# One-hot matrices of two MoE routings: eight blocks by one broadcast comparison on VectorE, the products with the codes on GpSimd

## The chip, the cores and the metric

The kernel runs on one core of a Trainium2 chip. The metric is the device time of one execution in microseconds (us). The engines of the core that matter here are TensorE (PE, with its weight loads PEld), VectorE (DVE), ScalarE (ACT), GpSimd (POOL) and the queues that issue DMAs (SP's, and POOL's for indirect ones). Each runs its own list of instructions in order; they meet through semaphores.

## The reference

Two transformer-like layers in a row on x of shape [2, 2048, 128], each half followed by a residual and a layer norm:

```python
x = layernorm(x + deltanet(x))          # layer 0: short convolution, 4 heads, chunks of 64
x = layernorm(x + moe_top1(x))          # 8 experts, GELU, width 512: only the chosen expert counts
x = layernorm(x + linear_attention(x))  # layer 1: 16 heads, causal, no softmax
x = layernorm(x + moe_top2(x))          # 8 experts, SiLU gate * up, width 256, the two largest logits
```

In `moe_top1` a token's output is that of the expert with the largest router logit, times its softmax probability; in `moe_top2` it is the sum over the two chosen experts, weighted by the softmax of their two logits.

## The kernel before

There are 4096 tokens, in `BLOCKS` = 32 blocks of 128. A token lies in a partition, a block in a column. Both mixtures of experts work on sorted tokens: `single_experts` (layer 0) makes `TILES` = 39 tiles of 128 rows, each of one expert; `stage_pairs` (layer 1) makes `GR` = 46 tiles, each of two halves of 64 rows, each half of one pair of experts. Before its tiles can be computed, each finds out which token goes into which row of which tile. That is the routing. It runs once in each layer, while almost nothing else runs:

1. VectorE finds the expert (or the pair) of each token and writes a selection matrix `sel`; TensorE counts tokens by expert and block (`ps_count`), VectorE and TensorE turn the counts into the place of each token, `slot`.
2. VectorE splits `slot` into a tile number `col` and a row in the tile `pos` (L1237 to L1239, L2114 to L2116).
3. For each of the 32 blocks VectorE writes two small matrices with one row per token: `at_pos`, one-hot over 128 rows, and `at_col`, the token's number (`code`) in the column of its tile and 0 elsewhere (39 or 46 columns). TensorE multiplies the two and adds up over the blocks in `ps_found`, which then holds, for each row of each tile, the number of its token. This loop is the one that the diff rewrites:

```python
for n in range(BLOCKS):
    v.tensor_scalar(at_pos[:, n], pos_no[:, :], pos[:, n:n + 1], None, ALU.is_equal)
    v.tensor_scalar(at_col[:, n], col_no[:, :], col[:, n:n + 1], code[:, n:n + 1], ALU.is_equal, ALU.mult).then_inc(hot, 1)
```

4. TensorE waits for `hot` block by block. After the last block VectorE turns `ps_found` into the addresses `read_at` (L1244; in layer 1 L2121 to L2125 also `write_at`) and increments `decoded`. It then works out each tile's experts, TensorE packs them into words (`ps_words`, with the matrix `pack`), and VectorE copies them (`words`), which releases the expert loops of all engines (`read`).
5. GpSimd gathers the rows of each tile by indirect DMA from `xe_dram` (L1094, L1909). For that it waits for `decoded` and for `stored`: the whole of `xe` is written to `xe_dram` by one DMA of SP's queue (L1044, L1852), started when the routing weights are in `xe`.

GpSimd also makes the constants (iota, memset, affine_select). The semaphore `const` counts them: at 2 (layer 0) or 3 (layer 1) all that the routing needs is there but `pack`, which 8 (or 4) more small instructions finish (L1088, L1893). In the kernel before, TensorE ahead of its counts (L1106, L1928) and VectorE (L1223, L2095) wait for all of them.

In layer 0 each engine has, between its part of the routing and the next, a piece of preparation for the linear attention: `ready(pe)` and `ready(pool)` call `ready_tensor` and `ready_gpsimd`. GpSimd's part ends with seven instructions on small matrices, L1401 to L1413, of which TensorE needs `centre` (L1404) and `bo_mat` (L1411) in its own preparation (L1469 to L1480), which stands ahead of its 32 matmuls of the one-hot matrices.

The helper `spread(ap, n)` repeats each element n times (step 0 in the innermost dimension); `every(ap, n)` repeats the whole row n times (step 0 in an outer one). `link` increments a semaphore and waits for it on VectorE.

Of the kernel before, what the change touches and what calls it, by code (L numbers as in the profile page):

```python
# [9 lines left out]
ALU = mybir.AluOpType  # L10
# [3 lines left out]
P = 128  # L14
B, L, D = 2, 2048, 128
BLOCKS = B * L // P
# [15 lines left out]
def spread(ap, n):  # L32

    return ap.unsqueeze(len(ap.shape)).broadcast_to([*ap.shape, n])
# [913 lines left out]
F16 = mybir.dt.float16  # L948
# [3 lines left out]
GR = (B * L + PAIRS * (HALF - 1)) // P + 1  # L952
ROUND = float(3 * 2 ** 22)
# [14 lines left out]

TILES = (B * L + E * (P - 1)) // P


def single_experts(nc, io, sb, tag, st, banks, w_in, wa, wb, b2):
# [3 lines left out]
    PACK = 8  # L976
# [19 lines left out]
    count, ends, first, one = (tmp(n, [P, E]) for n in ("count", "ends", "first", "one"))  # L996
    slot, col, pos = (tmp(n, [P, BLOCKS]) for n in ("slot", "col", "pos"))
    col_no, pos_no, code = tmp("col_no", [P, TILES]), tmp("pos_no", [P, P], F16), tmp("code", [P, BLOCKS])
    at_pos, at_col = tmp("at_pos", [P, BLOCKS, P], F16), tmp("at_col", [P, BLOCKS, TILES], F16)
# [18 lines left out]
    b1_in, b1_ps, b1_done, y_done, ranked = (sem(n) for n in ("b1_in", "b1_ps", "b1_done", "y_done", "ranked"))  # L1018
    row_in = [sem(f"row_in{i}") for i in range(ROWS)]
# [49 lines left out]
    def gpsimd(pool, ready):  # L1069
# [26 lines left out]

        ready(pool)
        pool.wait_ge(decoded, 1)
        pool.wait_ge(stored, 16)
# [102 lines left out]
    def vector(dve):  # L1202
        v = nc.vector
        links = 0

        def link(ins):

            nonlocal links
            links += 1
            ins.then_inc(step, 1)  # L1210
            dve.wait_ge(step, links)
# [25 lines left out]
        link(v.tensor_scalar(col[:, :], slot[:, :], 1.0 / P, -127 / 256, ALU.mult, ALU.add))  # L1237
        link(v.tensor_scalar(col[:, :], col[:, :], ROUND, -ROUND, ALU.add, ALU.add))
        link(v.scalar_tensor_tensor(pos[:, :], col[:, :], -float(P), slot[:, :], ALU.mult, ALU.add))  # L1239
# [527 lines left out]
def stage_pairs(nc, io, sb, tag, v_in, wac, wb):  # L1767
# [7 lines left out]
    with ExitStack() as st:  # L1775
        def tmp(name, shp, dt=F32):
            return st.enter_context(nc.sbuf_tensor(f"{tag}_{name}", shp, dt))

        def sem(name):
            return take(nc, f"{tag}_{name}")  # L1780

        def bank(name, shp):
# [16 lines left out]
        halves, ends, first, one = (tmp(n, [P, PAIRS]) for n in ("halves", "ends", "first", "one"))  # L1799
        slot, col, pos = (tmp(n, [P, BLOCKS]) for n in ("slot", "col", "pos"))  # L1800
        col_no, pos_no, code = tmp("col_no", [P, GR]), tmp("pos_no", [P, P], F16), tmp("code", [P, BLOCKS])
        at_pos, at_col = tmp("at_pos", [P, BLOCKS, P], F16), tmp("at_col", [P, BLOCKS, GR], F16)
# [20 lines left out]
            "hot", "found", "decoded", "paired", "packed", "read", "stored", "bias_in"))  # L1823
        ranked = sem("ranked")
        row_in = [sem(f"row_in{i}") for i in range(ROWS)]
# [6 lines left out]
        def every(ap, n):  # L1832

            return ap.unsqueeze(1).broadcast_to([ap.shape[0], n, ap.shape[1]])
# [12 lines left out]
        with nc.Block(no_gpsimd_drain=True) as block:  # L1847
# [19 lines left out]
            def _(pool):  # L1867
# [44 lines left out]
                def scatter(g):  # L1912
                    pool.wait_ge(n_done, g + 1)
                    pool.indirect_dma_start(out=out, out_offset=bass.IndirectOffsetOnAxis(ap=write_at[:, g:g + 1], axis=0),  # L1914
                                            in_=z[:, g], in_offset=None, bounds_check=B * L - 1, oob_is_err=False).then_inc(sent, 16)

                pool.wait_ge(decoded, 2)
                pool.wait_ge(stored, 16)
# [8 lines left out]
            def _(pe):  # L1927
                pe.wait_ge(const, 7)  # L1928
                pe.wait_ge(selected, 1)
# [12 lines left out]
                for n in range(BLOCKS):  # L1942
                    pe.wait_ge(hot, n + 1)
                    mm = nc.tensor.matmul(ps_found, at_pos[:, n], at_col[:, n], start=(n == 0), stop=(n == BLOCKS - 1))
                mm.then_inc(found, 1)
                pe.wait_ge(paired, 1)
                pe.wait_ge(decoded, 2)
                nc.tensor.matmul(ps_words, both[:, :], pack[:, :], start=True, stop=True).then_inc(packed, 1)
# [114 lines left out]
            def _(dve):  # L2063
# [30 lines left out]
                link(v.scalar_tensor_tensor(pair[:, :], hi[:, :], 0.5, lo[:, :], ALU.mult, ALU.subtract))  # L2094
                dve.wait_ge(const, 7)  # L2095
                v.tensor_tensor(sel[:, :, :], every(pair_no[:, :], BLOCKS), spread(pair[:, :], PAIRS), ALU.is_equal).then_inc(selected, 1)  # L2096
# [17 lines left out]
                link(v.tensor_scalar(col[:, :], slot[:, :], 1.0 / P, -127 / 256, ALU.mult, ALU.add))  # L2114
                link(v.tensor_scalar(col[:, :], col[:, :], ROUND, -ROUND, ALU.add, ALU.add))
                link(v.scalar_tensor_tensor(pos[:, :], col[:, :], -float(P), slot[:, :], ALU.mult, ALU.add))  # L2116
                for n in range(BLOCKS):
                    v.tensor_scalar(at_pos[:, n], pos_no[:, :], pos[:, n:n + 1], None, ALU.is_equal)  # L2118
                    v.tensor_scalar(at_col[:, n], col_no[:, :], col[:, n:n + 1], code[:, n:n + 1], ALU.is_equal, ALU.mult).then_inc(hot, 1)  # L2119
                dve.wait_ge(found, 1)  # L2120
# [127 lines left out]
```

## Time and profile before

| | us |
|---|---|
| median of 3 runs | 779.83 |
| the runs | 779.83, 772.3, 779.96 |
| the profiled execution, its own time | 777.14 |
| its span, first to last instruction | 775.4 |
| TensorE, VectorE, ScalarE, GpSimd busy | 618.8, 425.0, 351.9, 286.6 |
| mean granted TensorE clock | 0.854 |

The span is what the trace shows; 1.74 us of the execution lie around it. Busy shares are means over stages of different kinds; the two routings are short stages, at about 285 to 308 us and 551 to 585 us of the span, so it is the order of events there that has to be read.

### The profile page before, as it was taken

Reading aid. Unit: us, or ns where it says so; the run is one execution under the profiler, and the core shown is the slowest. Engines: PE = TensorE matmul, PEld = TensorE weight load, DVE = VectorE, ACT = ScalarE, POOL = GpSimd, SP = SyncE. Lnnn points to the kernel's source line nnn. Section 1 sums busy time; section 2 is a strip of 40 time slices with the busy share of each in tenths; the row PEclk is TensorE's granted clock in tenths of the full one; section 3 lists DMA queues with packets and bytes.
Section 4 is the critical chain, followed back from the end, with each engine's and each line's share of the span. In section 5 each row is a group of like instructions: output and inputs, shape, how many; then the busy total and the mean of one; then the engine's idle time right before and its main releaser. Section 6 shows DMA issues by size and latency. Waiting matters only on the chain. (4 is left out here: it accounts for less than half of the span.)

```text
span 775.4 us, 40316 instructions
## 1 busy us (share of the span) xinstructions
PE 618.8 (80%) x16699; PEld 466.9 (60%) x16699; DVE 425.0 (55%) x1490; ACT 351.9 (45%) x935; POOL 286.6 (37%) x489
## 2 busy tenths in 40 slices
PE   4787545999998935899939899998147999999993
PEld 3665445988888923899926667666122455554552
DVE  4996370133332568155543546657594667767765
ACT  4764110222222660578843454644104555665562
POOL 2244302122211453444325336353404255455434
PEclk9997555799999685799976999999556999999997
DMA  4011112222222916566521111100063333333430
GB/s 122 2 39 39 38 54 71 71 91 92 92 85 76 339 53 123 173 194 210 171 62 46 36 28 37 30 27 8 1 110 82 94 102 110 100 100 106 104 96 12
DMA packets 70850, 66.45 MB, mean 86 GB/s; under 512 B 17183, under 2 KB 60366, under 8 KB 70512
## 3 DMA queue, kind: packets, MB, share of 16 engines
q1 hardware_dynamic: 65488, 55.43, 23.5%
q0 software_dynamic: 5280, 10.00, 6.1%
q8 instruction: 42, 0.69, 0.4%
q14 instruction: 40, 0.33, 0.2%
HBM read 20.70 MB, written 11.93 MB: 42 GB/s over the span
## 5 line engine op out<-in xcount | busy, mean ns | idle before, releaser
L1962 PE MATMUL e_psH<-wac,e_xT 128*64 x184 | 91.4, 620 | 0.8 <-ACT e_xT L2022 0.6
L1964 PE MATMUL e_psH<-e_up_w,e_xT 128*64 128x512 f32 x184 | 91.4, 621 | 0.0
L1909 POOL DMA_INDIRECT e_row<-xe_dram,e_read_at x46 | 44.6, 970 | 73.7 <-DVE spare L2150 45.3
L1914 POOL DMA_INDIRECT out<-spare,e_write_at x46 | 46.3, 1007 | 47.3 <-ACT spare L2039 36.9
L596 POOL TENSOR_TENSOR tb<-tinv,mb 128x128 f32<-128x128 f32 x64 | 24.3, 401 | 85.4 <-PE d_psY L610 85.4
L1094 POOL DMA_INDIRECT e_row<-xe_dram,e_read_at x39 | 37.0, 948 | 49.4 <-DVE spare L1258 34.6
L2143 DVE TENSOR_TENSOR e_h<-e_pre,e_psH 128x512 f32<-128x512 f32 x46 | 31.6, 687 | 42.9 <-ACT e_pre L2028 42.9
L2028 ACT ACTIVATE e_pre<-e_psH 128x512 f32<-128x512 f32 x46 | 27.5, 598 | 58.4 <-PE e_psH L1964 57.9
L1983 PE MATMUL e_psY<-vb,e_hT 128*64 x368 | 50.8, 282 | 2.9 <-issue 2.9
L1180 ACT ACTIVATE e_hT<-mid_ps,e_b 128x128 f32<-128x128 f32 x156 | 45.0, 381 | 15.1 <-PE mid_ps L1136 14.9
L1986 PE MATMUL e_psY<-e_down_w,e_hT 128*64 128x128 f32 x368 | 50.8, 282 | 0.0
L721 DVE TENSOR_TENSOR S<-d_psS,on 128x64 f32<-128x64 f32 x64 | 14.3, 223 | 60.7 <-PE d_psS L667 60.7
L1983 PEld LDWEIGHTS e_psY<-vb,e_hT 128*64 128x64 f32 x368 | 39.6, 138 | 10.7 <-issue 10.7
L1136 PE MATMUL mid_ps<-e_xT,e_up_w 128*128 128x128 f32 x312 | 44.4, 289 | 0.2 <-DMA e_up_w<-wa 0.2
L2016 ACT ACTIVATE e_up_w<-wac 128x512 f32 x46 | 28.8, 626 | 33.4 <-DVE e_words L2137 26.9
L1962 PEld LDWEIGHTS e_psH<-wac,e_xT 128*64 128x64 f32 x184 | 22.0, 139 | 34.4 <-issue 29.9
L1144 PE MATMUL mid_ps<-wb,e_hT 128*128 x312 | 42.2, 280 | 0.5 <-issue 0.4
L1973 PEld LDWEIGHTS e_psT<-ident,e_h 128*128 128x128 f32 x184 | 19.3, 140 | 36.7 <-issue 36.5
L1662 DVE TENSOR_TENSOR a_sc<-mid_ps,a_tri 128x512 f32<-128x512 f32 x64 | 40.9, 680 | 0.0
L1136 PEld LDWEIGHTS mid_ps<-e_xT,e_up_w 128*128 128x128 f32 x312 | 40.4, 202 | 0.6 <-issue 0.4
L1986 PEld LDWEIGHTS e_psY<-e_down_w,e_hT 128*64 128x64 f32 x368 | 39.6, 138 | 0.0
L1144 PEld LDWEIGHTS mid_ps<-wb,e_hT 128*128 128x128 f32 x312 | 38.7, 196 | 1.2 <-issue 1.0
(386 smaller groups left out, 1778.7 us busy)
## 6 DMA issues: line engine op xcount, KB each, us to landing
e_down_w<-vb SPq DMA_DIRECT2D x92, 128.0 KB, 2.0
e_up_w<-wa SPq DMA_DIRECT2D x39, 256.0 KB
xe_dram<-xe SPq DMA_DIRECT2D x2, 2080.0 KB, 13.2
vk_now<-vk SPq DMA_DIRECT2D x18, 192.0 KB, 2.1
kq_now<-kq SPq DMA_DIRECT2D x18, 192.0 KB, 2.1
gk_now<-gk SPq DMA_DIRECT2D x18, 128.0 KB, 2.0
outs_dram<-spare SPq DMA_DIRECT2D x9, 256.0 KB, 2.8
r<-in_L_attn_hidden_states SPq DMA_DIRECT2D x8, 256.0 KB, 4.6
```

The source lines that it names most:

```text
L1094: pool.indirect_dma_start(out=row[g % ROWS][:, :], out_offset=None, in_=x_dram, in_offset=bass.IndirectOffsetOnAxis(ap=read_at[:, g:g + 1] ...
L1136: mm = nc.tensor.matmul(psH[g % 2][:, f], up_w[g % DEEP][:, f * P:(f + 1) * P], xT[g % 2][:, :], start=True, stop=True)
L1144: mm = nc.tensor.matmul(psY[g % 2][:, 0:D], hT[g % DEEP][:, f], wb[:, bass.ds(who * NF + f, 1)].rearrange("p a d -> p (a d)"), start=(f == ...
L1180: act.activation(hT[g % DEEP][:, f], psH[g % 2][:, f], ACT.Gelu, bias=b1[:, bass.ds(who * NF + f, 1)]).then_inc(h_done, 1)
L1662: ins = v.tensor_tensor(sc[:, g].rearrange("p k h l -> p (k h) l"), psS[g][:, :].rearrange("p (a l) -> p a l", l=HALF_T), tri[:, :].unsque ...
L1909: pool.indirect_dma_start(out=row[g % ROWS][:, :], out_offset=None, in_=x_dram, in_offset=bass.IndirectOffsetOnAxis(ap=read_at[:, g:g + 1] ...
L1914: pool.indirect_dma_start(out=out, out_offset=bass.IndirectOffsetOnAxis(ap=write_at[:, g:g + 1], axis=0), in_=z[:, g], in_offset=None, bou ...
L1962: nc.tensor.matmul(psH[g % 2][0:HALF, j], xT[g % 2][:, 0:HALF], wac[:, bass.ds(who[0][j], 1)].rearrange("p a f -> p (a f)"), start=True, s ...
L1964: mm = nc.tensor.matmul(psH[g % 2][HALF:P, j], xT[g % 2][:, HALF:P], up_w[g % 2][j][:, :], start=True, stop=True)
L1983: nc.tensor.matmul(psY[0:HALF, j], hT[g % 2][:, j, k * P:k * P + HALF], wb[:, bass.ds(who[0][j] * NF + k, 1)].rearrange("p a d -> p (a d)" ...
L1986: mm = nc.tensor.matmul(psY[HALF:P, j], hT[g % 2][:, j, k * P + HALF:(k + 1) * P], down_w[g % DEEP][:, j, k], start=(k == 0), stop=(k == N ...
L2143: v.tensor_tensor(h[g % 2][:, :, :], pre[g % 2][:, :, :], psH[g % 2][:, :, F:2 * F], ALU.mult).then_inc(h_done, 1)
```

## The change

In each of the two routings the 64 small VectorE instructions become 8 large ones, and 4 instructions come onto GpSimd. `pos`, `col` (now `at`), `code` and `col_no` become 16-bit (F16) tensors. VectorE compares eight blocks at a time, first for `at_col` (semaphore `matched`), then for `at_pos` (`hot`); it only writes ones and zeros. GpSimd multiplies `at_col` in place with the codes (`col_hot`), and TensorE waits for both before each eighth matmul. The waits for `pack` move behind the one-hot matmuls. The core of the diff, for layer 0 (layer 1 is the same, with `GR` for `TILES`, `const` 3 and 7 for 2 and 2 + `PACK`, and `decoded` 2):

```diff
+AHEAD = 8
-    col_no, pos_no, code = tmp("col_no", [P, TILES]), tmp("pos_no", [P, P], F16), tmp("code", [P, BLOCKS])
+    at, pos = tmp("at", [P, BLOCKS], F16), tmp("pos", [P, BLOCKS], F16)
+    col_no, pos_no, code = tmp("col_no", [P, TILES], F16), tmp("pos_no", [P, P], F16), tmp("code", [P, BLOCKS], F16)
# GpSimd
         ready(pool)
+        for c in range(BLOCKS // AHEAD):
+            s = slice(c * AHEAD, (c + 1) * AHEAD)
+            pool.wait_ge(matched, c + 1)
+            pool.tensor_tensor(at_col[:, s], at_col[:, s], spread(code[:, s], TILES), ALU.mult).then_inc(col_hot, 1)
         pool.wait_ge(decoded, 1)
# TensorE
-        pe.wait_ge(const, 2 + PACK)
+        pe.wait_ge(const, 2)
         pe.wait_ge(selected, 1)
...
         for n in range(BLOCKS):
-            pe.wait_ge(hot, n + 1)
+            if n % AHEAD == 0:
+                pe.wait_ge(hot, n // AHEAD + 1)
+                pe.wait_ge(col_hot, n // AHEAD + 1)
             mm = nc.tensor.matmul(ps_found, at_pos[:, n], at_col[:, n], start=(n == 0), stop=(n == BLOCKS - 1))
         mm.then_inc(found, 1)
         pe.wait_ge(numbered, 1)
+        pe.wait_ge(const, 2 + PACK)
         pe.wait_ge(decoded, 1)
# VectorE
-        dve.wait_ge(const, 2 + PACK)
+        dve.wait_ge(const, 2)
...
-        for n in range(BLOCKS):
-            v.tensor_scalar(at_pos[:, n], pos_no[:, :], pos[:, n:n + 1], None, ALU.is_equal)
-            v.tensor_scalar(at_col[:, n], col_no[:, :], col[:, n:n + 1], code[:, n:n + 1], ALU.is_equal, ALU.mult).then_inc(hot, 1)
+        for c in range(BLOCKS // AHEAD):
+            s = slice(c * AHEAD, (c + 1) * AHEAD)
+            v.tensor_tensor(at_col[:, s], every(col_no[:, :], AHEAD), spread(at[:, s], TILES), ALU.is_equal).then_inc(matched, 1)
+            v.tensor_tensor(at_pos[:, s], every(pos_no[:, :], AHEAD), spread(pos[:, s], P), ALU.is_equal).then_inc(hot, 1)
```

## Rows read from the trace of the kernel before

**Rows 1.** The page, chain that ended last: shares of the span by engine.

```profile
PE 23%; DVE 4%; issue 1%; DMA 1%; POOL 0%; ACT 0%; POOLq 0%; DVEq 0%
```

**Rows 2.** By tile: instructions, duration in ns (least, median, most), first and last start.

```profile
L2118 DVE TENSOR_SCALAR e_at_pos<-e_pos_no,e_pos x32: 246/253/258, 569.5 to 581.2; 128x128 f16<-128x128 f16 x32
...
L1242 DVE TENSOR_SCALAR e_at_col<-e_col_no,e_col,e_code x32: 299/305/314, 295.1 to 306.6; 128x39 f16<-128x39 f32 x32
...
L2119 DVE TENSOR_SCALAR e_at_col<-e_col_no,e_col,e_code x32: 300/306/311, 569.6 to 581.3; 128x46 f16<-128x46 f32 x32
```

**Rows 3.** Timeline, behind the loops: start, duration, engine, line, then idle before.

```profile
307.20 0.20 DVE L1244 TENSOR_SCALAR e_read_at<-mid_ps 128x39 uint32<-128x39 f32 x1 [0.31 <-PE mid_ps L1118]
...
581.94 0.21 DVE L2121 TENSOR_SCALAR e_late<-e_psR 128x46 f32<-128x46 f32 x1 [0.32 <-PE e_psR L1944]
```

**Rows 4.** Timeline, GpSimd: the first gathers of the two layers.

```profile
307.70 1.20 POOL L1094 DMA_INDIRECT e_row<-xe_dram,e_read_at  x1 [12.38 <-DVE e_read_at L1244]
...
583.12 1.07 POOL L1909 DMA_INDIRECT e_row<-xe_dram,e_read_at  x1 [21.02 <-DVE e_write_at L2125]
```

**Rows 5.** By line: the stores of xe, start and time from issue to landing.

```profile
L1044 SPq DMA_DIRECT2D xe_dram<-xe x1: 377/377/377, 290.7 to 290.7; - x1
...
DMA to landing us min/median/max: 13.9/13.9/13.9
...
L1852 SPq DMA_DIRECT2D xe_dram<-xe x1: 365/365/365, 562.1 to 562.1; - x1
...
DMA to landing us min/median/max: 12.6/12.6/12.6
```

**Rows 6.** Timeline, 287.6 to 291.7 us: the wait for `pack` in layer 0.

```profile
287.64 2.76 POOL L1088 TENSOR_SCALAR_AFFINE_SELECT e_pack<-e_pack 128x5 bf16<-128x5 bf16 x8
...
287.91 0.43 DVE L1219 TENSOR_TENSOR e_sel<-e_rank,e_key 128x256 f16<-128x256 f32 x1
...
290.46 0.64 PE L1109 MATMUL mid_ps<-e_ones,e_sel 128*32 128x1 f16 x8 [3.01 <-POOL e_pack L1088]
...
291.22 0.42 DVE L1225 TENSOR_TENSOR e_upto<-mid_ps,e_tri 32x264 f16<-32x264 f32 x1 [2.16 <-PE mid_ps L1109]
```

**Rows 7.** By form: a VectorE comparison of 256 elements (busy us, mean ns).

```profile
L2076 DVE TENSOR_TENSOR e_eq<-logits,e_top 128x256 f32<-128x256 f32 x2 | 0.8, 425 | 0.1
```

**Rows 8.** Timeline, 559.7 to 561.2 us: VectorE and GpSimd side by side.

```profile
559.75 0.27 POOL L1900 TENSOR_TENSOR xe<-xe,e_is_a 128x32 f32<-128x32 f32 x1
559.89 1.09 DVE L2096 TENSOR_TENSOR e_sel<-e_pair_no,e_pair 128x896 f16<-128x896 f32 x1
559.97 1.15 POOL L1900 TENSOR_TENSOR xe<-xe,e_is_b 128x32 f32<-128x32 f32 x1
560.90 0.25 DVE L2098 TENSOR_SCALAR e_den<-e_ex 128x32 f32<-128x32 f32 x1
```

**Rows 9.** By form: GpSimd's multiplications and additions (busy us, mean ns).

```profile
L596 POOL TENSOR_TENSOR tb<-tinv,mb 128x128 f32<-128x128 f32 x64 | 24.3, 401 | 85.4 <-PE d_psY L610 85.4
...
L1433 POOL TENSOR_TENSOR a_xb<-xe,a_b_o 128x256 f32<-128x256 f32 x16 | 10.8, 678 | 0.0
...
L202 POOL TENSOR_TENSOR ga<-gk,mb 128x256 f32<-128x256 f32 x8 | 5.0, 628 | 7.8 <-ACT gk L314 7.8
```

**Rows 10.** Timeline, 267.0 to 268.3 us: GpSimd first, VectorE second.

```profile
266.99 1.28 POOL L809 TENSOR_TENSOR f_og<-spare 128x512 f32<-128x512 f32 x1 [2.04 <-DVE f_oo L916]
...
267.77 0.52 DVE L930 TENSOR_TENSOR f_shift<-r,f_rstd 128x4 f32<-128x4 f32 x1
```

**Rows 11.** Timeline, TensorE: four one-hot matmuls that had queued up.

```profile
296.30 0.45 PE L1118 MATMUL mid_ps<-e_at_col,e_at_pos 128*128 128x39 f16 x4
```

**Rows 12.** Timeline, GpSimd: the end of its preparation in layer 0.

```profile
292.86 0.45 POOL L1403 TENSOR_SCALAR a_tri_b<-a_tri_b,a_low 128x64 f32<-128x64 f32 x1
...
295.01 0.31 POOL L1413 TENSOR_SCALAR a_bqm<-a_mr,a_bq 128x4 f32<-128x4 f32 x1
```

**Rows 13.** The page, granted TensorE clock in 40 slices of 19.4 us.

```profile
PEclk9997555799999685799976999999556999999997
```

More of the change, by code:

```diff
@@ L996, in single_experts @@
     count, ends, first, one = (tmp(n, [P, E]) for n in ("count", "ends", "first", "one"))
-    slot, col, pos = (tmp(n, [P, BLOCKS]) for n in ("slot", "col", "pos"))
-    col_no, pos_no, code = tmp("col_no", [P, TILES]), tmp("pos_no", [P, P], F16), tmp("code", [P, BLOCKS])
+    slot, col = tmp("slot", [P, BLOCKS]), tmp("col", [P, BLOCKS])
+    at, pos = tmp("at", [P, BLOCKS], F16), tmp("pos", [P, BLOCKS], F16)
+    col_no, pos_no, code = tmp("col_no", [P, TILES], F16), tmp("pos_no", [P, P], F16), tmp("code", [P, BLOCKS], F16)
     at_pos, at_col = tmp("at_pos", [P, BLOCKS, P], F16), tmp("at_col", [P, BLOCKS, TILES], F16)
@@ L1017, in single_experts @@
         "read", "stored"))
-    b1_in, b1_ps, b1_done, y_done, ranked = (sem(n) for n in ("b1_in", "b1_ps", "b1_done", "y_done", "ranked"))
+    b1_in, b1_ps, b1_done, y_done, ranked, matched = (sem(n) for n in ("b1_in", "b1_ps", "b1_done", "y_done", "ranked", "matched"))
+    col_hot = sem("col_hot")
     row_in = [sem(f"row_in{i}") for i in range(ROWS)]
@@ L1237, in vector @@
         link(v.tensor_scalar(col[:, :], slot[:, :], 1.0 / P, -127 / 256, ALU.mult, ALU.add))
[L1238 to L1242 removed]
+        link(v.tensor_scalar(at[:, :], col[:, :], ROUND, -ROUND, ALU.add, ALU.add))
+        link(v.scalar_tensor_tensor(pos[:, :], at[:, :], -float(P), slot[:, :], ALU.mult, ALU.add))
+        for c in range(BLOCKS // AHEAD):
+            s = slice(c * AHEAD, (c + 1) * AHEAD)
+            v.tensor_tensor(at_col[:, s], every(col_no[:, :], AHEAD), spread(at[:, s], TILES), ALU.is_equal).then_inc(matched, 1)
+            v.tensor_tensor(at_pos[:, s], every(pos_no[:, :], AHEAD), spread(pos[:, s], P), ALU.is_equal).then_inc(hot, 1)
         dve.wait_ge(found, 1)
@@ L1799, in stage_pairs @@
         halves, ends, first, one = (tmp(n, [P, PAIRS]) for n in ("halves", "ends", "first", "one"))
-        slot, col, pos = (tmp(n, [P, BLOCKS]) for n in ("slot", "col", "pos"))
-        col_no, pos_no, code = tmp("col_no", [P, GR]), tmp("pos_no", [P, P], F16), tmp("code", [P, BLOCKS])
+        slot, col = tmp("slot", [P, BLOCKS]), tmp("col", [P, BLOCKS])
+        at, pos = tmp("at", [P, BLOCKS], F16), tmp("pos", [P, BLOCKS], F16)
+        col_no, pos_no, code = tmp("col_no", [P, GR], F16), tmp("pos_no", [P, P], F16), tmp("code", [P, BLOCKS], F16)
         at_pos, at_col = tmp("at_pos", [P, BLOCKS, P], F16), tmp("at_col", [P, BLOCKS, GR], F16)
@@ L1823, in stage_pairs @@
             "hot", "found", "decoded", "paired", "packed", "read", "stored", "bias_in"))
-        ranked = sem("ranked")
+        ranked, matched = sem("ranked"), sem("matched")
+        col_hot = sem("col_hot")
         row_in = [sem(f"row_in{i}") for i in range(ROWS)]
@@ L1915, in scatter @@
                                             in_=z[:, g], in_offset=None, bounds_check=B * L - 1, oob_is_err=False).then_inc(sent, 16)
+                for c in range(BLOCKS // AHEAD):
+                    s = slice(c * AHEAD, (c + 1) * AHEAD)
+                    pool.wait_ge(matched, c + 1)
+                    pool.tensor_tensor(at_col[:, s], at_col[:, s], spread(code[:, s], GR), ALU.mult).then_inc(col_hot, 1)
                 pool.wait_ge(decoded, 2)
@@ L1927, in _ @@
             def _(pe):
-                pe.wait_ge(const, 7)
+                pe.wait_ge(const, 3)
                 pe.wait_ge(selected, 1)
@@ L1942, in _ @@
                 for n in range(BLOCKS):
-                    pe.wait_ge(hot, n + 1)
+                    if n % AHEAD == 0:
+                        pe.wait_ge(hot, n // AHEAD + 1)
+                        pe.wait_ge(col_hot, n // AHEAD + 1)
                     mm = nc.tensor.matmul(ps_found, at_pos[:, n], at_col[:, n], start=(n == 0), stop=(n == BLOCKS - 1))
@@ L1946, in _ @@
                 pe.wait_ge(paired, 1)
+                pe.wait_ge(const, 7)
                 pe.wait_ge(decoded, 2)
@@ L2094, in _ @@
                 link(v.scalar_tensor_tensor(pair[:, :], hi[:, :], 0.5, lo[:, :], ALU.mult, ALU.subtract))
-                dve.wait_ge(const, 7)
+                dve.wait_ge(const, 3)
                 v.tensor_tensor(sel[:, :, :], every(pair_no[:, :], BLOCKS), spread(pair[:, :], PAIRS), ALU.is_equal).then_inc(selected, 1)
@@ L2114, in _ @@
                 link(v.tensor_scalar(col[:, :], slot[:, :], 1.0 / P, -127 / 256, ALU.mult, ALU.add))
[L2115 to L2119, printed above, removed]
+                link(v.tensor_scalar(at[:, :], col[:, :], ROUND, -ROUND, ALU.add, ALU.add))
+                link(v.scalar_tensor_tensor(pos[:, :], at[:, :], -float(P), slot[:, :], ALU.mult, ALU.add))
+                for c in range(BLOCKS // AHEAD):
+                    s = slice(c * AHEAD, (c + 1) * AHEAD)
+                    v.tensor_tensor(at_col[:, s], every(col_no[:, :], AHEAD), spread(at[:, s], GR), ALU.is_equal).then_inc(matched, 1)
+                    v.tensor_tensor(at_pos[:, s], every(pos_no[:, :], AHEAD), spread(pos[:, s], P), ALU.is_equal).then_inc(hot, 1)
                 dve.wait_ge(found, 1)
```

## The prediction

> **What bounds the kernel now.** I read the chain of waits first. TensorE leads it, and VectorE has 4% of the span [rows 1], about 31 us. Most of those lie where the edits are: nothing else can go on while a routing runs, so what shortens a routing shortens the kernel one for one, up to the next wait. The by-tile view shows what a routing spends on its one-hot matrices: in layer 1 the pairs of `at_pos` and `at_col` start from 569.5 to 581.3 us, 32 of them every 0.38 us; the last ends at 581.63. In layer 0 they run from 294.9 to 306.9 [rows 2]. So each loop takes 12.0 to 12.2 us, and VectorE sits still only 0.31 us more, for the last matmul, before it decodes [rows 3]. The durations of 0.25 and 0.31 us overlap; the step of 0.38 counts. GpSimd's first gathers start 0.5 us after the decode in layer 0 and 1.2 us after it in layer 1 [rows 4]. They have a second condition: the store of `xe` lands at 290.7 + 13.9 = 304.6 us and at 562.1 + 12.6 = 574.7 us [rows 5]. It is hidden now, by 3.1 and 8.4 us; in layer 0 that is a floor under what the change can give.
>
> **The waits for `pack`.** In layer 0 `sel` is written at 288.34, but TensorE's counts start at 290.46, when the eight `pack` instructions that began at 287.64 are done [rows 6]. `const` was at 2 before 287.64, so with the change the counts start at about 288.4: 2.06 us earlier. VectorE's `upto` follows, and so does the whole chain up to `pos`; the first comparison moves from 294.9 to about 292.8. `pack` is needed only behind `decoded`, over 10 us after it is done, so the moved wait costs nothing. In layer 1 the routing reaches its wait at 559.9 [rows 8], and `pack` has by then long been finished (four instructions of some 0.3 us, started with the stage); the edit gives 0 there.
>
> **VectorE's comparisons.** Two rows of the same form with f32 operands: 256 elements take 0.425 us [rows 7], 896 take 1.09 [rows 8]. That is 1.04 ns an element and 0.16 us for the instruction, of which 0.08 overlaps the next (the next starts at 560.90 where the comparison ends at 560.98). The row of 896 even has the form of the new ones: a row repeated as one operand, an element repeated as the other, f16 out. By it `at_pos` of eight blocks (1024 elements) is 1.15 us from start to start, `at_col` 0.46 in layer 1 (368) and 0.40 in layer 0 (312). A group is 1.61 or 1.55 us, four are 6.5 and 6.3 with the last end, against 12.2 and 12.0. No row has a comparison with 16-bit operands. The ends: as f32, or half the time an element (0.08 + 0.53 and 0.08 + 0.19, four groups 3.6 us). I take the first, because the form is that of the row.
>
> The Trainium skill speaks both ways here. "VectorE: DVE Perf Modes", in its perf-mode tier table, gives a 16-bit `tensor_tensor` two elements a cycle, by which the sum would be that of the third rival below. "Vector Engine (DVE) Microarchitecture Reference" § 5.1 wants a step of one in the innermost dimension of every operand, and reports one element for all cycles where an element is read again and again, as `spread` does; by it the sum stays as it is. No row of this trace decides.
>
> **GpSimd's products.** A multiplication with one operand repeated takes 0.401 us for 128 elements and 0.628 for 256; a plain addition 0.678 for 256 [rows 9] and about 1.27 for 512 [rows 10]. From the first two (the same form) 368 elements make 0.83 us and 312 make 0.73; from the other two, 0.94 and 0.81. All are f32 and none is f16 or in place, so the upper end is open: I allow twice, 1.7 us, and for the lower end 0.6.
>
> **They don't run side by side.** This decides the sum. GpSimd's multiplication of 32 elements takes 0.27 us; the next, the same in size, starts 0.08 us after VectorE's comparison of 896 and takes 1.15, ending 0.14 us behind it [rows 8]. The other way round, a VectorE operation of 4 elements that begins inside GpSimd's of 512 takes 0.52 us and ends 0.02 us after it [rows 10]. So with two inputs in SBUF on both engines, whoever comes second stands still until the first is done; some 0.13 us of its start (0.27 less 0.14) is hidden meanwhile. Each product becomes ready when `at_pos` of its own group has just begun, and its turn comes after. Whether VectorE lets it in between its instructions or not, the times add up: 6.5 + 4 x (0.83 - 0.12) = 9.4 us in layer 1, instead of 12.2.
>
> **The tail on TensorE.** Now one matmul follows the last comparison; then it will be eight. Four that had queued up took 0.45 us [rows 11], one takes 0.22, so a further one costs 0.08 and eight 0.78 us. With the semaphore the decode starts 0.87 us after the last product, against 0.31 now: 0.56 lost.
>
> **Layer 1:** 12.16 - 9.4 - 0.56 = 2.2 us. The decode comes at 579.7, behind the store (574.7). GpSimd has nothing else to do there.
>
> **Layer 0.** GpSimd still has its preparation to do when the comparisons begin: seven instructions, from 292.86 to 295.32 [rows 12], all reading SBUF. Now they meet the new comparisons at 292.8. They add up too: 6.3 (comparisons) + some 2.0 (the seven, 2.46 less part of their starts) + 4 x 0.61 (products) = 10.7, so the last product ends at 303.5 and the decode starts at 304.4, 2.8 us earlier. The gather then waits for the store until 304.6. Also, TensorE's preparation needs two of the seven and then has 32 matmuls (2.6 us) to catch up; they start 3.4 us after the first of the seven now [rows 11, 12]. If GpSimd only gets in once VectorE is done at 299.1, they start near 302.5 and the decode comes at 305.2, 2.0 us earlier. I take 2.5 us.
>
> **Sum.** 2.5 + 2.2 = 4.7 us. Behind the routings all is shifted, not changed: `read`, the gathers, the weight loads hang on it. The granted clock is 5 tenths, that is 1.2 GHz, in the slices of both routings [rows 13] and stays there with less work. The profiled execution took 777.14 us, 2.7 less than the median of the three runs; the four executions have a mean of 777.3 and lie 7.7 apart, so I start from that mean: 777.3 - 4.7 = 772.6 us. About 1%, 7.8 us, is what a measurement of this kernel can tell from no change.
>
> **Rivals.**
> - *No contention with 16-bit operands.* Then the products hide behind the comparisons. Layer 1: the last comparison ends 6.5 us after the first, the eight matmuls follow, 12.2 - 6.5 - 0.56 = 5.1 us. Layer 0 is cut off by the store at 3.0. Together 8.1: 769.2 us. Against it: rows 8 and 10, both ways. Chance 0.10.
> - *Slower: the product on GpSimd.* A multiplication in place with f16 in and out, in rows of 39 or 46 with a stride-0 code, may be no stream at the f32 rate. VectorE and TensorE wait for it eight times and nothing covers it, since VectorE is held up as well. The gain is gone when a product takes 0.8 + 4.7/8 = 1.4 us; at 2.1 us the kernel loses 8 x 1.3 - 4.7 = 5.7 us: 783.0. For it: no f16 row of GpSimd with two inputs. Against it: the rate of the f32 rows is steady. Chance 0.08.
> - *16-bit comparisons at twice the rate.* Four groups take 3.6 us. Layer 1: 12.2 - 3.6 - 2.8 - 0.56 = 5.2; layer 0 at the store's floor, 3.0: 8.2 us, 769.1. This is what the first page named above makes of it. Chance 0.12.
> - *The change does nothing.* Each handing over of the port costs 0.1 to 0.2 us more than I think (eight or more a routing), and layer 0 is bound by TensorE's preparation: 1 to 2 us are left, 776. Chance 0.15.
>
> My forecast has the remaining 0.55.
>
> **Range and chances.** The forecast alone, with product costs of 0.6 to 1.0 us, is 770 to 775; single executions scatter by 3 to 4 us around their mean. The range takes in the fast rivals and that scatter: 766 to 780. Faster by over 1% than the median (under 772.0): about a third of the forecast's chance by scatter, most of the two fast rivals: 0.35. Slower by over 1%: only the slow product at its worst, 0.04. Within 1%: 0.61.
>
> **What would show it.** Right: in layer 0 the counts start near 288.4; `at_pos` rows last 1.2 us and `at_col` rows 0.5; GpSimd's product rows last far over 0.8 us where they overlap a comparison, or VectorE's comparisons last longer than their elements explain; eight matmuls in under 1 us behind the last product; the first gathers near 305 and 578.5. Wrong: `at_pos` rows of 0.7 us (twice the rate); products of 0.8 us beside comparisons of normal length (no contention); products of 1.5 us and more with VectorE idle; a gather that waits for the store in layer 1; a clock that comes back later in the tile loops than before.

## The result, and the profile after

The changed kernel takes 770.96 us (median of 20 runs, 765.94 to 777.73), the kernel before 779.68 (median of as many runs). The ratio on record is 0.9932, with a 95% interval of 0.9904 to 0.9959: a gain of 0.7%, 5.3 us, between 3.2 and 7.5. It compares fast executions with fast ones, since some executions run in a slower state; one of the changed kernel (777.73) counts as such. The two medians lie further apart than the ratio says, 8.7 us, and the two means 7.4 (without one execution of the kernel before that took 999.18); nothing on record explains the difference. I go by the ratio, because the stages below and a second measurement on another chip (5.4 us between the medians, e8) agree with it. The profiled execution took 775.07 us against 777.14, so the two profiles lie only 2.1 us apart. They can't be compared by their ends; they have to be compared stage by stage. I take three times of each routing, counted from GpSimd's first instruction in it (the iota of `rank`, at 285.57 and 551.01 us before, 286.11 and 554.06 after): the first comparison, the decode, and the first gather, from which on everything is only shifted.

| us from the start of the routing | before | after | gain | predicted |
|---|---|---|---|---|
| layer 0: first comparison | 9.32 | 7.27 | 2.05 | 2.1 |
| layer 0: decode | 21.63 | 17.26 | 4.37 | 2.0 to 2.8 |
| layer 0: first gather | 22.13 | 20.44 | 1.69 | 2.5 |
| layer 1: first comparison | 18.46 | 18.45 | 0.01 | 0 |
| layer 1: decode | 30.93 | 28.01 | 2.92 | 2.2 |
| layer 1: first gather | 32.11 | 29.19 | 2.92 | 2.2 |

The two gains make 4.6 us, inside the interval of the ratio. The rest of the span, whose code is the same, differs too: 0.5 us more ahead of layer 0's routing, 4.2 more between the routings and 2.1 less behind layer 1's, together 2.6 us the other way. So the profiles show only 2.0 of the 4.6.

The page of the changed kernel: busy times, and the granted clock in 40 slices, to be laid beside [rows 13].

```profile
PE 607.4 (79%) x16699; PEld 461.6 (60%) x16699; DVE 415.5 (54%) x1378; ACT 351.7 (45%) x935; POOL 299.5 (39%) x497
...
PEclk9988555799999585899967899999557999999997
```

VectorE has lost 9.5 us of busy time and GpSimd has gained 12.9. The products are 9.6 us, though they are only 2720 elements per partition in both layers; the seven preparation instructions of layer 0 last 4.2 longer, and the rest of GpSimd's work 0.9 less. The granted clock is still at 5 tenths (1.2 GHz) in both routings, as it was.

The timeline of layer 1 after: start, duration, engine, line, idle before. It answers to the second row of rows 3 and of rows 4.

```profile
572.51 0.54 DVE L2139 TENSOR_TENSOR e_at_col<-e_col_no,e_at 128x368 f16<-128x368 f16 x1
572.97 1.22 DVE L2140 TENSOR_TENSOR e_at_pos<-e_pos_no,e_pos 128x1024 f16<-128x1024 f16 x1
573.13 1.72 POOL L1933 TENSOR_TENSOR e_at_col<-e_at_col,e_code 128x368 f16<-128x368 f16 x1 [7.99 <-DVE e_at_col L2139]
574.11 1.14 DVE L2139 TENSOR_TENSOR e_at_col<-e_col_no,e_at 128x368 f16<-128x368 f16 x1
...
575.17 1.21 DVE L2140 TENSOR_TENSOR e_at_pos<-e_pos_no,e_pos 128x1024 f16<-128x1024 f16 x1
...
579.71 1.71 POOL L1933 TENSOR_TENSOR e_at_col<-e_at_col,e_code 128x368 f16<-128x368 f16 x1 [0.48 <-DVE e_at_col L2139]
...
581.57 0.47 PE L1963 MATMUL e_psR<-e_at_col,e_at_pos 128*128 128x46 f16 x8 [1.72 <-POOL e_at_col L1933]
582.07 0.21 DVE L2142 TENSOR_SCALAR e_late<-e_psR 128x46 f32<-128x46 f32 x1 [1.30 <-PE e_psR L1963]
...
583.25 1.06 POOL L1922 DMA_INDIRECT e_row<-xe_dram,e_read_at  x1 [1.83 <-DVE e_write_at L2146]
```

Read the ends, not the starts. The first product starts at 573.13, 0.16 us into `at_pos`, and ends at 574.85, 0.66 us after `at_pos` does (574.19). The next `at_col`, free to start at 574.11, takes 1.14 us where the first one took 0.54. It ends at 575.25, 0.40 behind the product. The two engines take turns, instruction by instruction, and a long bar is mostly waiting. The by-tile view shows the pattern in all four groups (duration in ns: least, median, most):

```profile
L2139 DVE TENSOR_TENSOR e_at_col<-e_col_no,e_at x4: 541/1132/1137, 572.5 to 578.5; 128x368 f16<-128x368 f16 x4
L1933 POOL TENSOR_TENSOR e_at_col<-e_at_col,e_code x4: 1712/1714/1715, 573.1 to 579.7; 128x368 f16<-128x368 f16 x4
```

The first `at_col` has nobody to wait for and takes 541 ns; the others take about 1132. The timeline of layer 0:

```profile
289.03 0.61 PE L1116 MATMUL mid_ps<-e_ones,e_sel 128*32 128x1 f16 x8 [1.03 <-POOL e_pack L1091]
...
293.45 1.79 POOL L1414 TENSOR_SCALAR a_tri_b<-a_tri_b,a_low 128x64 f32<-128x64 f32 x1
293.78 1.22 DVE L1253 TENSOR_TENSOR e_at_pos<-e_pos_no,e_pos 128x1024 f16<-128x1024 f16 x1
...
298.63 1.30 DVE L1253 TENSOR_TENSOR e_at_pos<-e_pos_no,e_pos 128x1024 f16<-128x1024 f16 x1
298.85 1.25 POOL L1424 TENSOR_SCALAR a_bqm<-a_mr,a_bq 128x4 f32<-128x4 f32 x1
...
300.07 2.69 POOL L1104 TENSOR_TENSOR e_at_col<-e_at_col,e_code 128x312 f16<-128x312 f16 x4
...
303.37 0.20 DVE L1255 TENSOR_SCALAR e_read_at<-mid_ps 128x39 uint32<-128x39 f32 x1 [3.44 <-PE mid_ps L1127]
...
306.55 1.20 POOL L1097 DMA_INDIRECT e_row<-xe_dram,e_read_at  x1 [3.78 <-DMA xe_dram<-xe]
```

TensorE's counts start 2.92 us into the stage, against 4.89 before [rows 6]. The releaser named in that row is the `pack` instruction that ended last before it; it is inferred, and what the counts really waited for is `sel`, written by 288.89.

GpSimd spends all of the comparisons on its seven preparation instructions: from 293.45 to 300.10, where it took 2.46 us before [rows 12]. An operation on 64 elements now takes 1.79 us and one on 4 elements 1.25. The products come only when VectorE has finished, and so run undisturbed, four in 2.69 us. Then comes the row that matters: the gather waits 3.78 us for the store. The store, by its line:

```profile
L1047 SPq DMA_DIRECT2D xe_dram<-xe x1: 377/377/377, 291.3 to 291.3; - x1
...
DMA to landing us min/median/max: 14.4/14.4/14.4
```

It is issued as long after the stage's start as before (5.17 us against 5.13), lands 14.4 us later at 305.7 (13.9 before, [rows 5]), and the gather starts 0.85 us behind that. The decode came 4.4 us earlier; the gather gained 1.7 of them.

### The profile page after: what moved, and what is told of

Same layout as the page of the kernel before. It is cut to its first block and busy times, and to the rows that moved or that the text cites. A ratio compares the mean times of both kernels' runs of the same rounds, so it can differ in the third digit from the quotient of the medians.

```text
span 773.4 us, 40220 instructions
## 1 busy us (share of the span) xinstructions
PE 607.4 (79%) x16699; PEld 461.6 (60%) x16699; DVE 415.5 (54%) x1378; ACT 351.7 (45%) x935; POOL 299.5 (39%) x497
```

## The experiments

They ran on two other chips, on which the kernel before takes 818.4 us (25 runs, beside e1 to e4) and 818.5 (11 runs, beside e5 to e8). The columns of stage lengths are from one profile each. So each time stands against the kernel before on the same chip, and stages are compared by their lengths, which hardly change: the changed kernel has 20.53 and 29.20 us to its first gathers there (e8), 20.44 and 29.19 in the profile above. All in one table; the gathers are counted from the stage's start:

| | median, us (runs) | ratio to before, 95% | layer 0: decode / gather | layer 1: gather |
|---|---|---|---|---|
| before (profile above) | 818.4 | 1 | 21.63 / 22.13 | 32.11 |
| e1 the waits alone | 815.45 (10) | 0.9963 (0.9928 to 0.9998) | 19.82 / 20.33 | 32.04 |
| e7 the loops alone | 816.69 (1) | one run | 18.24 / 20.69 | 29.16 |
| e8 the changed kernel | 813.14 (6) | 0.9921 (0.9892 to 0.9949) | 17.26 / 20.53 | 29.20 |
| e4 products on VectorE | 812.5 (10) | 0.9913 (0.9878 to 0.9948) | 16.02 / 19.86 | 28.54 |
| e2 constants in PSUM | 811.28 (10) | 0.9916 (0.9881 to 0.9951) | 15.68 / 20.09 | 26.59 |
| e3 other layout | 806.03 (4) | 0.9849 (0.9782 to 0.9915) | 14.26 / 20.25 | 24.88 |
| e5 e3, store by ScalarE | 805.15 (6) | 0.984 (0.9806 to 0.9874) | 17.12 / 19.09 | 24.89 |
| e6 e3, store in two parts | 812.11 (1) | one run | 24.05 / 24.55 | 24.87 |

### e1: the waits alone

```diff
 # the kernel before; TensorE and VectorE, layer 0 (layer 1: 7 to 3)
-        pe.wait_ge(const, 2 + PACK)
+        pe.wait_ge(const, 2)
...
-        dve.wait_ge(const, 2 + PACK)
+        dve.wait_ge(const, 2)
...
         pe.wait_ge(numbered, 1)
+        pe.wait_ge(const, 2 + PACK)
```

> The kernel before with the moved waits for pack alone; the 64 small VectorE instructions stay. I measure each routing from GpSimd's first iota to its first gather: 22.1 us (layer 0) and 32.1 us (layer 1) before, 20.4 and 29.2 after the change. If the store of xe is what ends layer 0's routing now, this edit alone reaches the floor: decode 2.06 us earlier, layer 0 at 20.1 to 20.5, so that the rewritten loop adds nothing to it there. Layer 1 stays at 32.1. Whole time about 1.7 us (0.2%) under before. Rival, that the rewritten loop is what shortens layer 0: 21.5 or more here.

What the gather waited for (us in all, times, longest):

```profile
POOL e_row L1094 <- DVE e_read_at L1245: 10.6, 1, 10.6
```

Two waits moved, and layer 0's gather comes at 20.33 us instead of 22.13, as early as with the whole change. It still waits for the decode. The store landed 13.9 us after its issue at 288.2, 19.1 us into the stage, so with the 0.85 us seen above it would have let the gather go at about 20.0: this edit alone has used up nearly all that the store leaves. Layer 1 doesn't move, as predicted. The whole time is 3.0 us lower for 1.7 expected; the interval, 0.2 to 5.9 us, holds both.

### e7: the loops alone

```diff
 # the changed kernel, layer 0
-        pe.wait_ge(const, 2)
+        pe.wait_ge(const, 2 + PACK)
...
-        dve.wait_ge(const, 2)
+        dve.wait_ge(const, 2 + PACK)
```

> The changed kernel with the old waits for pack: the rewritten comparisons and products alone. Layer 0: the first comparison back from 7.3 to 9.3 us after the first iota, the decode from 17.3 to about 19; the store lands about 20, so first iota to first gather is still 20.0 to 20.5 us: either half of the change reaches the floor of layer 0 by itself. Rival, that the halves add up there: 22 us. Layer 1 at 29.2, as changed.

```profile
POOL e_row L1097 <- DMA xe_dram<-xe: 3.1, 1, 3.1
```

The other half alone gives 20.69. In layer 0 the halves are worth 1.8 and 1.4 us, and together 1.6 to 1.7: they don't add up, because both run into the same DMA. With the waits moved, the new loops give the kernel the 2.9 us of layer 1 and nothing in layer 0. Where the gather waits for the store and SP issues it as before, its place follows the store's own time: 19.86 us with a store of 13.8 (e4), 20.09 with 14.0 (e2), 20.25 with 14.2 (e3), 20.53 with 14.5 (e8), 20.69 with 14.6 here. These differences say nothing of the edits.

The run shows one thing more about the moved waits. They bring the first comparison 2.1 us forward, but the decode only 1.0 (18.24 to 17.26): from the first comparison to the decode it is 8.91 us here and 9.99 with the whole change. Here six of GpSimd's seven preparation instructions are over, or within 0.1 us of it, when the comparisons begin; with the waits moved all seven fall among the comparisons, and the products come behind them.

### e8: the changed kernel again

> The changed kernel again, on the chip of these runs, to stand beside e5_act_store: layer 0 20.4, layer 1 29.2 us; against the kernel before 0.993 to 0.995, e5_act_store 6 us (0.8%) under it.

It repeats the first measurement (0.9932) within its interval. e5 has a median 8.0 us under this one, where 6 were expected; the two routings account for 5.8 of it. The runs also bear on the 4.2 us that the two first profiles differ by between the routings: that stretch, with identical code, is 264.1 to 269.1 us long in the eight profiles of this section (267.85 in e8; 267.80 in e1 and 267.60 in e7). It varies by up to 5 us from profile to profile, so the 4.2 are best taken as scatter; one profile of each kernel can't prove it.

### e4: the products on VectorE

```diff
 # GpSimd: the four products are gone
 # VectorE, both loops
             v.tensor_tensor(at_pos[:, s], every(pos_no[:, :], AHEAD), spread(pos[:, s], P), ALU.is_equal).then_inc(hot, 1)
+            dve.wait_ge(matched, c + 1)
+            v.tensor_tensor(at_col[:, s], at_col[:, s], spread(code[:, s], TILES), ALU.mult).then_inc(col_hot, 1)
```

> The changed kernel with the products on VectorE, in the same layout, and none on GpSimd. If the two engines exclude each other, GpSimd's product costs 0.85 us of VectorE's time and VectorE's own costs 0.46, so taking it back is no loss: four groups take 8.3 us instead of 8.9, layer 1 goes from 29.2 to about 28.6, layer 0 stays at the store. If GpSimd did work beside VectorE, layer 1 would get longer, by up to 4 x 0.46 = 1.8 us, to 31.0.

By tile, layer 1's products:

```profile
L2136 DVE TENSOR_TENSOR e_at_col<-e_at_col,e_code x4: 533/534/535, 587.6 to 593.7; 128x368 f16<-128x368 f16 x4
```

GpSimd's help was none. A product on VectorE takes 0.534 us, 0.45 from start to start, against the 0.61 that it adds to a group when GpSimd does it; layer 1 is 0.66 us shorter without the second engine. The ratios of e4 and e8 can't be told apart; the stage lengths can.

### e2: the same instructions, the constants in PSUM

ScalarE copies `pos_no` and `col_no` into a PSUM bank that is free at this time, and VectorE reads them there. GpSimd's products stay.

```diff
+        act.activation(pos_ps, pos_no[:, :], ACT.Copy)
+        act.activation(col_ps, col_no[:, :], ACT.Copy).then_inc(filled, 1)
...
+        dve.wait_ge(filled, 1)
...
-            v.tensor_tensor(at_pos[:, s], every(pos_no[:, :], AHEAD), spread(pos[:, s], P), ALU.is_equal).then_inc(hot, 1)
+            v.tensor_tensor(at_pos[:, s], every(pos_ps, AHEAD), spread(pos[:, s], P), ALU.is_equal).then_inc(hot, 1)
```

> The changed kernel, with the two constant rows that VectorE compares against copied once to PSUM by ScalarE, so that each comparison has one input in SBUF instead of two. If two inputs in SBUF on both engines exclude each other, nothing stands still any more in layer 1: the products last 0.85 us instead of 1.71, the at_col comparisons 0.54 instead of 1.13, and the last comparison ends 6.5 us after the first; layer 1 goes from 29.2 to 27.0 us. Layer 0 stays at the store, 20.4, with an earlier decode (about 300). If the long rows are what a 16-bit product and comparison cost by themselves, both stay long and layer 1 stays at 29.2.

By tile, layer 1:

```profile
L2152 DVE TENSOR_TENSOR e_at_pos<-e_psH,e_pos x4: 1215/1215/1215, 587.8 to 592.5; 128x1024 f16<-128x1024 f32 x4
...
L2151 DVE TENSOR_TENSOR e_at_col<-e_psH,e_at x4: 531/531/541, 587.3 to 592.1; 128x368 f16<-128x368 f32 x4
L1941 POOL TENSOR_TENSOR e_at_col<-e_at_col,e_code x4: 801/801/801, 587.9 to 592.7; 128x368 f16<-128x368 f16 x4
```

This is the experiment that shows the mechanism in layer 1. The product falls from 1714 to 801 ns, the later comparisons of `at_col` from 1132 to 531, and `at_pos` keeps its 1.21 us. What changed is where one operand of VectorE lies. With the move it also became f32, but the type isn't what frees the engines: with f32 operands in SBUF they held each other up in the kernel before [rows 8]. The groups are 1.58 us apart instead of 2.19, and layer 1's gather comes at 26.59 us, 2.6 earlier (27.0 us expected). In the three rows neither engine holds up the other. The Trainium skill says so in "SBUF — State Buffer", section "Who interferes with whom": a VectorE instruction with two inputs in SBUF contends with a GpSimd instruction that reads SBUF, and one with at most one SBUF input does not, outside the modes in which VectorE uses both of its port pairs for a single input. The runs agree on both halves, by 1714 against 801 ns.

Layer 0 has a price that layer 1 hasn't: the first comparison comes 8.97 us into the stage instead of 7.27. Of these 1.70 us, 0.4 come from ScalarE's exponentials, which the copies delay by 1.6 us and for which VectorE waits, and 1.1 from one VectorE instruction of 8 elements:

```profile
288.54 1.28 DVE L1243 TENSOR_SCALAR e_count<-e_count 128x8 f32<-128x8 f32 x1
288.79 1.00 POOL L1411 MEMSET a_vm<- 128x1088 f32 x1
```

The same instruction takes 0.17 us in the changed kernel, where the memset isn't under way. Here it ends 0.03 us behind the memset. It has one input in SBUF; if the memset held it, a single input is no safeguard for every kind of instruction. That is read from these two rows, and no run isolates it.

### e3: no repeated element innermost

The one-hot matrices are laid out with four blocks innermost, so that the four block values, not one repeated value, are what VectorE reads side by side. The constants are written four times in a row. The products are on VectorE, as in e4.

```diff
-    at_pos, at_col = tmp("at_pos", [P, BLOCKS, P], F16), tmp("at_col", [P, BLOCKS, TILES], F16)
+    at_pos, at_col = tmp("at_pos", [P, BLOCKS // K, P, K], F16), tmp("at_col", [P, BLOCKS // K, TILES, K], F16)
...
-            mm = nc.tensor.matmul(ps_found, at_pos[:, n], at_col[:, n], start=(n == 0), stop=(n == BLOCKS - 1))
+            mm = nc.tensor.matmul(ps_found, at_pos[:, n // K, :, n % K], at_col[:, n // K, :, n % K], start=(n == 0), stop=(n == BLOCKS - 1))
...
+            v.tensor_tensor(at_pos[:, q], twice(pos_no[:, :, :]), rows(pos[:, s], P), ALU.is_equal).then_inc(hot, 1)
 # K = 4; rows(): element step 1 over four blocks, repeated in an outer dimension; twice(): the constants for two such fours
```

> No product on GpSimd, and four blocks innermost in both matrices and both constants, so that every operand of VectorE's three operations by group has step 1 innermost and 16 bits; TensorE reads its operands with a step of four elements. If the step of 0 is what held the comparisons at one element a cycle, they now run at two: at_pos 0.69 us instead of 1.21, at_col and its product 0.35 each, a group 1.17 us, four 4.7 us instead of 8.9; layer 1 goes from 29.2 to 25.0, layer 0 stays at the store (20.4). If 16-bit comparisons run at one element a cycle whatever the step, at_pos stays at 1.21 and layer 1 is 28.6.

By tile, layer 1:

```profile
L2144 DVE TENSOR_TENSOR e_at_pos<-e_pos_no,e_pos x4: 684/684/686, 589.0 to 592.4; 128x1024 f16<-128x1024 f16 x4
...
L2143 DVE TENSOR_TENSOR e_at_col<-e_col_no,e_at x4: 344/344/350, 588.7 to 592.1; 128x368 f16<-128x368 f16 x4
L2146 DVE TENSOR_TENSOR e_at_col<-e_at_col,e_code x4: 341/343/344, 589.6 to 593.0; 128x368 f16<-128x368 f16 x4
```

The same 1024 comparisons of the same 16-bit type take 684 ns instead of 1213: without the fixed 0.15 us or so, half the time an element. That is what the third rival of the prediction wanted, and it needs the layout as well as the type. The two pages that the prediction weighed against each other thus both hold here, the first under the condition of the second: by the Trainium skill, "Vector Engine (DVE) Microarchitecture Reference" § 5.1, a repeated element gives the fast rate away, and the trace agrees, 1213 against 684 ns. TensorE pays a little for its operands lying four elements apart: eight queued matmuls take 0.53 us, against 0.47. Layer 1's gather comes 7.2 us earlier than before, 4.3 earlier than with the change. It is close to its own floor there: the store of layer 1 was issued at 581.4 us and landed 12.8 us later, so with the 0.85 us of layer 0 it would have let the gather go at about 595.05, and the gather started at 595.21. In layer 0 it is at 20.25, still at the floor:

```profile
POOL e_row L1107 <- DMA xe_dram<-xe: 7.7, 1, 7.7
```

### e5: e3, and the store from ScalarE's queue

In layer 0 SP issues the store behind eleven small loads, 5.2 us into the stage. Here ScalarE issues it.

```diff
 # SP, layer 0
-        sp.wait_ge(weighed, 1)
-        sp.wait_ge(const, 2)
-        sp.dma_start(x_dram.rearrange("(n p) c -> p n c", p=P), xe[:, :, :]).then_inc(stored, 16)
 # ScalarE
+        act.wait_ge(weighed, 1)
+        act.wait_ge(const, 2)
+        act.dma_start(x_dram.rearrange("(n p) c -> p n c", p=P), xe[:, :, :]).then_inc(stored, 16)
```

> e3_inner with the store of xe in layer 0 issued from ScalarE's queue as soon as the weights are there, not from SP's behind its ten loads. In e3_inner the decode is ready 6 us before the gather. If the landing of the store alone ends layer 0's routing, the 1.5 us or so by which the store starts earlier come back one for one: first iota to first gather 18.4 to 18.8 us instead of 20.2, layer 1 unchanged at 24.9. If something else holds the gather (GpSimd itself, the bandwidth that the loads and the store share), it stays at 20.

By line:

```profile
L1179 ACTq DMA_DIRECT2D xe_dram<-xe x1: 435/435/435, 285.4 to 285.4; - x1
...
DMA to landing us min/median/max: 14.7/14.7/14.7
```

The store is issued 3.5 us into the stage instead of 5.2 and takes 14.7 us instead of the 14.2 of e3; the gather comes at 19.09, 1.2 us earlier than in e3, where 1.4 to 1.8 were expected. The small loads that SP still issues come later now: GpSimd waits 3.3 us for the bias that `bo_mat` is made of, and the decode slips from 14.26 to 17.12. This hides here, because the gather waits for the store anyhow. It is the version with the lowest time, 1.6% (1.3 to 1.9) below the kernel before; the ratios of e3 and e5 can't be told apart, and what separates the two is layer 0's length.

### e6: e3, and the store in two parts

The 128 columns of x at the start of the stage, the two columns of weights where the store was.

```diff
+        sp.dma_start(x_dram.rearrange("(n p) c -> p n c", p=P)[:, :, 0:D], xe[:, :, 0:D]).then_inc(stored, 16)
         sp.dma_start(b1_rows[:, :], io["L0_ffn_b1"].rearrange("e (f p) -> (e f) p", p=P)).then_inc(b1_in, 16)
...
-        sp.dma_start(x_dram.rearrange("(n p) c -> p n c", p=P), xe[:, :, :]).then_inc(stored, 16)
-        sp.wait_ge(stored, 16)
+            sp.dma_start(x_dram.rearrange("(n p) c -> p n c", p=P)[:, :, D:], xe[:, :, D:]).then_inc(stored, 16)
+        sp.wait_ge(stored, 32)
```

> e3_inner with the store of layer 0 split: the 128 columns of x are stored at the start of the stage, since they are complete by then, and only the two columns of weights after the routing weights are known (4096 pieces of 8 bytes). If the store is the floor and small pieces are cheap, the large part lands near 14.5 and the small part soon behind: first iota to first gather 16 to 18 us. Rival: a piece of 8 bytes costs a DMA engine nearly as much as a row of 520 bytes, so that the second store takes nearly as long as the first and queues behind it: 24 us or more.

The timelines of SP's queue and TensorE:

```profile
282.27 0.38 SPq L1053 DMA_DIRECT2D xe_dram<-xe  x1
282.70 6.76 SPq L1054 DMA_DIRECT2D e_b_rows<-in_L_ffn_b  x1
289.50 0.42 SPq L1392 DMA_DIRECT2D a_w_raw<-in_L_attn_wq_w  x1
...
294.32 0.38 SPq L1059 DMA_DIRECT2D xe_dram<-xe  x1
```

```profile
296.69 0.31 PE L1120 MATMUL mid_ps<-ident,e_b_rows 32*128 32x32 f32 x1 [20.36 <-DMA e_b_rows<-in_L_ffn_b]
296.93 0.64 PE L1124 MATMUL mid_ps<-e_ones,e_sel 128*32 128x1 f16 x8
```

A miss. The first store took 14.2 us to its landing at 296.5, and the small load queued behind it (`b_rows`, L1054), whose issue alone took 6.76 us, was there only at about 296.7. TensorE stands in order at the transpose of just that load, with the counts behind it: they start at 296.93, the first comparison comes 19.03 us into the stage instead of 7.73, and the gather at 24.55. The store's second part, 32 KB in 4096 pieces of 8 bytes, was issued late for the same reason and took 9.8 us to land, at 304.1; the decode, later still, hid it. The gather's 24.55 us are the number of the rival ("24 us or more"), but not for its reason: the second store did not take as long as the first, and did not hold the gather. So the run shows what a large store in front of a small load costs. What the split by itself is worth, with the load ahead of the store, it does not show; that was not tried.

## Why the prediction came out right, and where it didn't

**What bounds it.** Right. A routing stands alone, and what shortens it up to its next wait shortens the kernel: gains of 4.6 us in the two stages, 5.3 (3.2 to 7.5) in the runs. The experiments agree: the stages gain 1.9, 7.6, 5.8, 9.1 and 10.3 us in e1, e2, e4, e3 and e5, and the ratios say 3.0, 6.9, 7.1, 12.4 and 13.1, each with the stages' gain inside its interval or, in e5, at its edge.

**The waits for `pack`.** Right as far as the comparisons: 2.05 us earlier for 2.1 predicted, nothing in layer 1 (e1: 32.04). That the moved wait costs nothing held as far as `pack` goes: its matmul never waited for it. The price that the prediction put under "Layer 0" is there, though: GpSimd's preparation now meets the comparisons, and of the 2.05 us the decode keeps about 1.0 (e7).

**The comparisons.** Right by its first end. 1024 elements take 1.14 us from start to start (1.15 predicted), 368 take 0.46 (0.46 predicted); four groups without contention are 6.41 us in e2 (587.31 to 593.72; 6.5 predicted). That 16 bits don't run at twice the rate in this layout has the reason that e3 shows.

**No work side by side.** Right in mechanism, as e2 shows for layer 1. In size it was off a little: the four products of layer 1 add 8.92 - 6.41 = 2.5 us to the path where 2.8 was forecast (0.63 each instead of 0.71); a product by itself takes 0.80 us rather than 0.83. With the comparisons, the last product ends 8.92 us after the first comparison began, not 9.4.

**The tail on TensorE.** The mechanism was right, the term over-sized. Eight queued matmuls take 0.47 us, not 0.78: in a queue of eight each further one costs (0.47 - 0.21)/7 = 0.04 us, where 0.08 was worked out from one group of four [rows 11]. That group had not all queued up. The comparison on which its fourth matmul waits, in the kernel before, is

```profile
296.18 0.30 DVE L1242 TENSOR_SCALAR e_at_col<-e_col_no,e_col,e_code 128x39 f16<-128x39 f32 x1
```

It ends at 296.48, when the group had begun at 296.30; so the 0.45 us of the row hold a wait for VectorE and not only the work of TensorE. The decode starts 0.64 us after the last product (581.43 to 582.07), not 0.87. This 0.23 and the 0.5 of the products and comparisons (9.4 - 8.92) are the 0.7 us by which layer 1 gained more than forecast.

**Layer 0.** The step that failed is "They add up too", in its second term, "some 2.0 (the seven, 2.46 less part of their starts)". The comparisons with the seven instructions of GpSimd among them took 6.55 us (293.38 to 299.93), against 6.17 in e2, where nothing held VectorE (292.58 to 298.75). So the seven cost VectorE 0.4 us, not 2.0, though they themselves took 6.65 instead of 2.46. They have 400 elements per partition in all, and 0.4 us is 1 ns for each. That fits an account in which the start of a waiting instruction lies beside VectorE's work and only its elements need the turn; no run tests this account by itself. The products, behind VectorE's last comparison and so with nothing of their starts hidden, end 2.83 us after it (2.4 predicted). With 0.61 us from there to the decode, the way from the first comparison to the decode is 6.55 + 2.83 + 0.61 = 10.0, instead of 11.6; it was 12.3 before. The decode gained 4.4 us for 2.0 to 2.8 forecast.

**The floor.** None of this came out, because the store's floor lay lower than I put it. I set the gather at the landing, 3.0 us ahead; it starts 0.85 us after that figure (up to 0.92 in the seven profiles where it waits for the store), and this store took 14.4 us instead of 13.9. The floor is 1.7 us away, and 1.7 was gained for 2.5. That the landing is the limit was said; that it is reached by either half of the change alone was not, and e1 and e7 show it.

**The rivals.** No contention: refuted by the products of 1714 ns; e2 shows what it would look like (products of 801 ns, groups of 1.58 us). A slow product on GpSimd: 0.80 us where nothing holds it up, and the f32 rows had given 0.83. Comparisons at twice the rate: not in this layout (e3). Nothing gained: each turn costs less than I allowed for, not more. The clock, which could have come back later, came back a little earlier in the profile of the changed kernel (a mean of 0.77 granted from 312 to 318 us, where the kernel before had 0.50); its gathers had also started 1.2 us earlier, and no run isolates the clock.

**Sum and start.** That the sum came out is luck: the two errors, +0.7 and -0.8, cancel, 4.6 for 4.7. The starting point, a mean of four executions (777.3), was 1.4 us under the mean of the 20 (about 778.7, one outlier left out), and the predicted 772.6 is 1.6 over the measured median. That closeness is luck too: from the median of the kernel before, 779.68, the same 4.7 us would have given 775.0. The measured median, 770.96, lies in the part of the range that had a chance of 0.35 (under 772.0), though the ratio on record is a gain of less than 1%. All of this is within the scatter, which goes with the granted clock: the fastest run, 765.94 us, had 0.881, those at 775 had 0.86.

## What to carry to other kernels

Before you move elementwise work to GpSimd to relieve VectorE, look where VectorE's operands lie: in these runs, with two of them in SBUF the engines take turns and the second one adds its time (a product of 1.71 us); with one in PSUM they run side by side (0.80 us). Time the copies to PSUM with care: in layer 0 of e2 they delayed ScalarE's next work by 1.6 us. A broadcast by a repeated innermost element kept 16-bit operands at the f32 rate (1213 ns for 1024 elements); with the repeated thing in an outer dimension the rate doubled (684 ns). That was worth 3.7 us in layer 1 (e4 to e3), where the second engine had cost 0.7. And ahead of shortening a chain, write down every other condition of its last instruction with its time: two edits that both reach the same DMA are worth as much as one, and the next gain is in issuing that DMA earlier, without putting anything small that is needed soon behind it.

## What was unexpected of the hardware

- Turns, and no starvation. In layer 0 VectorE had eight comparisons queued back to back, and GpSimd's seven short instructions still ended one by one (at 295.24, 295.83, 296.84, 297.24, 298.38, 298.86 and 300.10 us), only the last of them, begun at 298.85, after the end of the loop (299.93). TensorE's preparation was over at 299.5, before the first product was.
- Among the seven the price of taking turns fell on the side with few elements: 64 elements took 1.79 us instead of 0.45, while VectorE's 1024 went from 1.22 to 1.30 at most. Between instructions of like size both pay: in layer 1 368 elements took 1.71 us instead of 0.80 on GpSimd and 1.13 instead of 0.53 on VectorE, and in e7 one comparison of 1024 took 1.73.
- A comparison with one operand in PSUM, f32, and one in SBUF, f16, is as fast as with both in SBUF: 1215 against 1213 ns.
- The store of 2 MB took 13.8 to 14.7 us to land in layer 0 and 12.5 to 13.1 in layer 1, and a small load queued behind it wasn't there before it either (e6); the same load's issue took 6.76 us. A store of 32 KB in pieces of 8 bytes took 9.8 us.
